# Row scores in four 32-row array tiles, and turned scores from operands stacked over 128 partitions

## What is computed

```python
q = jnp.einsum('bse,ef->bsf', layernorm(x), Wq)       # 32 heads of 16
k = jnp.einsum('bse,ef->bsf', ctx, Wk)                # 8 heads of 16, each serves 4 query heads
v = jnp.einsum('bse,ef->bsf', ctx, Wv)
q, k = rope(q), rope(k)
scores = jnp.einsum('bhqd,bhkd->bhqk', q, repeat(k, 4)) * 0.25
x = x + jnp.einsum('bhqk,bhkd->bhqd', softmax(scores), repeat(v, 4)) @ Wo
h = layernorm(x)
gate = softmax over the 16 best of (h @ Wq_w.T @ keys.T), spread over 64 experts
x = x + ((h @ A_w.T) * repeat(gate, 8)) @ B_w.T * 2
```

## Time and profile before

| | |
|---|---|
| median of three runs | 170.12 us |
| span of the profiled execution | 168.1 us |
| outside the span (170.12 less 168.1) | 2.0 us |
| TensorE busy | 97% of the span |
| TensorE weight loads busy | 77% |
| VectorE busy | 80% |
| ScalarE busy | 53% |
| GpSimd busy | 54% |

### The profile page before, as it was taken

The page is one execution under the profiler, slowest core; times in us unless marked ns, Lnnn a source line. Parts: engine busy times, 40 slices in busy tenths (PEclk is TensorE's granted clock), DMA queues, the critical chain, the costliest instruction groups (busy, mean ns, idle before and its releaser), DMA issues.

```text
span 168.1 us, 4082 instructions
## 1 busy us (share of the span) xinstructions
PE 162.7 (97%) x1437; PEld 129.9 (77%) x1437; DVE 134.9 (80%) x394; ACT 89.8 (53%) x212; POOL 91.1 (54%) x113
## 2 busy tenths in 40 slices
PE   7999999899999999999999999999999999999993
PEld 2657786678878787879887987879888866889883
DVE  1969886986998899799887998699884988767752
ACT  3588989899656362723538234732349154333210
POOL 5479999899799654805952099206440303512100
DMA  5999952313203010210212000100010001000013
GB/s 173 361 415 388 408 161 62 129 21 105 66 7 118 4 62 0 78 52 0 64 59 69 4 0 0 64 4 0 0 66 0 0 4 62 4 0 4 0 62 125
DMA packets 6739, 13.46 MB, mean 80 GB/s; under 512 B 832, under 2 KB 1216, under 8 KB 6464
## 3 DMA queue, kind: packets, MB, share of 16 engines
q1 hardware_dynamic: 6432, 12.95, 22.7%
q10 hardware_dynamic: 288, 0.27, 0.5%
HBM read 11.11 MB, written 2.10 MB: 79 GB/s over the span
## 4 chain that ended last, share of the span: by engine, by line
PE 52%; POOL 26%; issue 11%; DVE 5%; ACT 2%; DMA 2%; POOLq 0%; ACTq 0%; DVEq 0%
PE ps_w L1234 8%; PE ps_w L1235 7%; PE ps_w L1239 7%; PE ps_t L1247 4%; POOL am_lo L330 3%; POOL k_bd_hi L374 3%; POOL wo_lo L330 3%; PE ps_s L1320 3%; PE ps_s L1339 3%; POOL wq_lo L330 3%; POOL b_lo L330 2%; PE ps_t L1234 2%; PE ps_t L1239 2%; PE ps_t L1235 2%; POOL k_bd_lo L374 2%
## 5 line engine op out<-in xcount | busy, mean ns | idle before, releaser
L921 DVE TENSOR_REDUCE ps_s<-ps_s 128x8 f32<-128x512 f32 x32 | 21.0, 689 | 0.6 <-PE ps_s L1320 0.3
L398 POOL TENSOR_TENSOR late<-late,gate 128x512 f32<-128x512 f32 x7 | 7.6, 1084 | 24.2 <-issue 17.3
L383 POOL TENSOR_TENSOR oT_lo<-o_n,oT_hi 128x512 fp32r<-128x512 f32 x8 | 10.4, 1296 | 15.7 <-ACT oT_hi L611 15.7
L603 ACT ACTIVATE eT<-ps_s 128x512 f32<-128x512 f32 x32 | 17.0, 600 | 3.4 <-PE ps_s L1345 3.4
L1234 PE MATMUL ps_w<-am_hi,x2T_hi 128*128 128x288 f32 x48 | 14.3, 320 | 0.0
L1235 PE MATMUL ps_w<-am_lo,x2T_hi 128*128 128x288 f32 x48 | 13.1, 295 | 0.0
L1234 PE MATMUL ps_w<-b_hi,zT_hi 128*128 128x512 f32 (+1 forms) x28 | 10.7, 389 | 0.0
L1227 PE MATMUL ps_w<-wq_hi,xT_hi 128*128 128x512 f32 x26 | 10.7, 411 | 0.0
L1234 PEld LDWEIGHTS ps_w<-am_hi,x2T_hi 128*128 128x128 f32 x48 | 9.0, 187 | 2.1 <-ACT late L635 0.4
L1235 PE MATMUL ps_w<-b_lo,zT_hi 128*128 128x512 f32 (+1 forms) x28 | 10.4, 376 | 0.0
L653 ACT ACTIVATE zT_hi<-ps_t 128x512 fp32r<-128x512 f32 x7 | 4.2, 598 | 11.4 <-PE ps_t L1247 11.4
(11 more groups left out here) (256 smaller groups left out, 537.2 us busy)
## 6 DMA issues: line engine op xcount, KB each, us to landing
x_sb<-x SPq DMA_DIRECT2D x8, 256.0 KB, 6.7
cT_in<-cT SPq DMA_DIRECT2D x7, 256.0 KB, 2.8
out<-res SPq DMA_DIRECT2D x7, 256.0 KB, 2.0
wq_sb<-wq SPq DMA_DIRECT2D x4, 256.0 KB, 5.4
late<-wo SPq DMA_DIRECT2D x1, 1024.0 KB, 7.7
am_sb<-aT SPq DMA_DIRECT2D x1, 1024.0 KB, 8.8
b_sb<-bT SPq DMA_DIRECT2D x1, 1024.0 KB, 7.2
xT_raw<-xT SPq DMA_DIRECT2D x4, 256.0 KB, 2.9
```

Source lines behind the costliest of these rows:

```text
L383: pool.tensor_tensor(oT_lo[:], o_n[:].rearrange("p (b r q) -> p r b q", b=2, r=REP), oT_hi[:].bitcast(F32), ALU.subtract).then_inc(oT_lo_o ...
L603: act.activation(eT[:, c].rearrange("p b n -> p (b n)"), ps_s[:, c, :], ACT.Exp)\
L921: dve.tensor_reduce(neg_top[:, b, HALF_H * half:HALF_H * (half + 1), :], ps_s[:, 2 * (1 - b) + half, :].rearrange("p (r h k) -> p h r k", ...
```

## The change

Row scores of tiles 0 to 6 (`quad_rows`): each product takes 32 rows (two heads) and 128 columns, four side by side, 48 a tile. The maxima are then taken over both head pairs of all four banks, and all four reductions wait until the scores of both sequences are there. `neg_top` moves to bank 0, and the reciprocals of tiles 0 to 2 leave `ps_s` for `inv_late`.

Turned scores of tiles 3 to 6 (`STACKED`): DMAs copy the 32 rows of each pair into one 128-row operand (`q_stack`: high, high, low, and the maxima; `k_stack`: high, low, high, and `sel`), and one full-array product stands for four. `m_out` writes the maxima straight into rows 96 to 127 of `q_stack`, once for each b. `turn_m` comes two weight chunks earlier in `late_step`. The stacks lie where `am_sb` and `b_sb` were.

```diff
+            def stack_sel():                  # SyncE
+                sp.wait_ge(am_l, DK)
+                sp.wait_ge(sel_ok, 2)
...
+                        sp.dma_start(k_stack[3 * QUAD:P, s, c].bitcast(F32),
+                                     sel[rows].bitcast(F32))\
+                          .then_inc(st_sel, 16)
+            def stack_k(t):
+                sp.wait_ge(k_bd_ok, 2 * t + 2)
+                if t - 2 in STACKED:
+                    sp.wait_ge(sT_ps, t - 1)
+                for c in range(PAIRS):
+                    rows, at = slice(QUAD * c, QUAD * (c + 1)), 2 * (c % 2)
+                    for n, part in enumerate((k_bd_hi, k_bd_lo, k_bd_hi)):
+                        sp.dma_start(k_stack[QUAD * n:QUAD * (n + 1), t % 2, c].bitcast(F32),
...
+            def stack_q(t):
+                sp.wait_ge(qT_lo_ok, t + 1)
+                if t - 1 in STACKED:
+                    sp.wait_ge(sT_ps, t)
+                else:
+                    sp.wait_ge(b_l, DK)
+                for c in range(PAIRS):
+                    for n, part in enumerate((qT_hi, qT_hi, qT_lo)):
+                        sp.dma_start(q_stack[QUAD * n:QUAD * (n + 1), c]...
...
             load_xT(5)
+            stack_k(3)
+            stack_q(3)
             load_c(6)
+            stack_k(4)
             store(0)
             load_xT(6)
+            stack_q(4)
             load_c(7)
+            stack_k(5)
             store(1)
             load_xT(7)
+            stack_q(5)
+            stack_k(6)
+            store(2)
+            stack_q(6)
...
             def m_out(t):                     # ScalarE
+                if t in STACKED:
+                    for b in range(2):
+                        act.activation(q_stack[3 * QUAD:P, :, b, :],
+                                       mT_bank(t)[3 * QUAD:P, :].unsqueeze(1).broadcast_to([QUAD, PAIRS, 2 * P]),
+                                       ACT.Copy).then_inc(mT_ok, 1)
+                    return
...
             def top(t, b):                    # VectorE
+                if quad_rows(t):
+                    if b == 0:
+                        dve.wait_ge(s_ps, 2 * t + 2)
+                        if t >= 1:
+                            dve.wait_ge(m_lo_ok, t)
+                    for rp in range(2):
...
+            def quad_scores(t):               # TensorE
+                pe.wait_ge(qT_hi_ok, t + 1)
+                pe.wait_ge(qT_lo_ok, t + 1)
+                pe.wait_ge(k_bd_ok, 2 * t + 2)
+                if t >= 1:
+                    pe.wait_ge(exp_ok, 4 * t)
+                    if not late_tile(t - 1):
+                        pe.wait_ge(o_step, 3 * t - 2)
+                for b in range(2):
+                    for rp in range(2):
+                        for n, (q, k) in enumerate(((qT_hi, k_bd_hi), (qT_hi, k_bd_lo), (qT_lo, k_bd_hi))):
+                            for c in range(PAIRS):
+                                rows = slice(QUAD * c, QUAD * (c + 1))
+                                mm = pe.matmul(ps_s[:, c, at:at + P], q[rows, ...], k[rows, ...],
+                                               start=(n == 0), stop=(n == 2))
+                mm.then_inc(s_ps, 2)
...
+            def stacked_scores(t):
+                pe.wait_ge(st_q[t], 16 * 3 * PAIRS)
+                pe.wait_ge(st_k[t], 16 * 3 * PAIRS)
+                pe.wait_ge(st_sel, 16 * 2 * PAIRS)
+                for b in range(2):
+                    for c in range(PAIRS):
+                        if b == 0 and c in (0, PAIRS - 1):
+                            pe.wait_ge(mT_ok, mT_count(t) - (c == 0))
+                        mm = pe.matmul(ps_s[:, c, 2 * P * b:2 * P * (b + 1)], k_stack[:, t % 2, c, b, :],
+                                       q_stack[:, c, b, :], start=True, stop=True)
+                mm.then_inc(sT_ps, 1)
...
             def late_step(i):
-                up_high(f)
+                up_high(f, [0, 1])
                 turn_m(n)
+                up_high(f, [2, 3])
                 up_low(f)
```

More of the change, by code:

```diff
@@ L158, in build, with mT_count, quad_rows, neg_top_of @@
         ROUTE = ps_s[:, :, 0:E]
+        def mT_count(t):
+            return t + 1 + sum(1 for s in STACKED if s <= t)
+        def quad_rows(t):
+            return t < T - 1
+        def neg_top_of(t):
+            if quad_rows(t):
+                return ps_s[:, 0, 0:4 * KVH].rearrange("p (r b h) -> p b h r", b=2, r=2)
+            return ps_s[:, 2, 0:4 * KVH].rearrange("p (b h r) -> p b h r", b=2, r=2)
         def z_bank(t, half):
@@ L250, in build @@
         up_ps, res_ok, stored = sem("up_ps"), sem("res_ok"), sem("stored")
+        st_q = {t: sem(f"st_q{t}") for t in STACKED}
+        st_k = {t: sem(f"st_k{t}") for t in STACKED}
+        st_sel = sem("st_sel")
         block = ctx.enter_context(nc.Block())
@@ L309, in _ @@
             load_c(5)
+            stack_sel()
             load_x(7)
             load_xT(5)
+            stack_k(3)
+            stack_q(3)
             load_c(6)
+            stack_k(4)
             store(0)
             load_xT(6)
+            stack_q(4)
             load_c(7)
+            stack_k(5)
             store(1)
             load_xT(7)
-            for t in range(2, T - 1):
+            stack_q(5)
+            stack_k(6)
+            store(2)
+            stack_q(6)
+            for t in range(3, T - 1):
                 store(t)
@@ L1311, in scores @@
                 if t >= 1:
-                    if b == 0 or late_tile(t - 1):
+                    if b == 0:
                         pe.wait_ge(exp_ok, 4 * t)
                     else:
-                        pe.wait_ge(o_step, 3 * t if t < T - 1 else 3 * t - 2)
+                        pe.wait_ge(o_step, 3 * t - 2)
                 for rp in range(2):
@@ L1331, in turn_m @@
                 mm.then_inc(m_ps, 1)
+            def stacked_scores(t):
[3 more added lines that the diff above has]
+                for b in range(2):
+                    for c in range(PAIRS):
+                        if b == 0 and c in (0, PAIRS - 1):
[3 more added lines that the diff above has]
+                mm.then_inc(sT_ps, 1)
             def turned_scores(t):
-                pe.wait_ge(mT_ok, t + 1)
+                if t in STACKED:
+                    stacked_scores(t)
+                    return
+                pe.wait_ge(mT_ok, mT_count(t))
                 for b in range(2):
@@ L1452, in first @@
                 pe.wait_ge(route_ok, 1)
-                scores(0, 0)
-                scores(0, 1)
+                quad_scores(0)
                 turn_k(1)
@@ L1475, in second @@
                 turn_xh(3)
-                scores(1, 0)
-                scores(1, 1)
+                quad_scores(1)
                 pe.wait_ge(v_st_ok, 3)
@@ L1511, in step @@
                     project_q(p, [2])
-                scores(n, 0)
-                scores(n, 1)
+                quad_scores(n)
                 if f >= 0:
```

42 lines of the change are left out of this document (34 added, 8 removed).

## The result

The changed kernel takes 173.6 us (median of four runs, 171.2 to 174.0) where the kernel before takes 170.0 (169.7 to 170.4): a ratio of 1.016, with a 95% interval of 1.009 to 1.024. Two things are to be explained, since the profiled execution is the fastest of the four: it took 171.2 us (span 169.5) with a granted clock of 1.00 throughout, the other three 173.6 to 174.0 with a mean clock of 0.99.

The account below looks back on a forecast made before the run. TensorE was taken to bound the late steps, VectorE's maxima the early ones. -1.6 - 0.25 + 0.58 + 0.31 = -0.96 us from a 168.1 us span gave 167.1, plus 2.0 for the median: 169.1 us, range 168.3 to 169.9.

Parts of the forecast that it names:

- Behind it stand the turn of the maxima and the turned scores of tile 1: Tile 1, behind VectorE's maxima 0.31 us late: work that TensorE reached just as it came, so the delay counts.
- The maxima: VectorE's reductions wait for both sequences' scores: +0.58 us on tile 0, +0.31 on tile 1, nothing from tile 2 on.
- Stacked scores: Turned scores, tiles 3 to 6: eight full-array products take 0.95 us, not 1.35, without shape-change bubbles; -0.40 a tile, -1.6 us.
- Row scores: Tiles 0 to 6: groups at 0.112 us, bound by weight loads, save 0.08 us a tile; -0.25 us, tiles 4 to 6.
- The rival in which weight loads don't bind: Row scores: groups take 0.063 us, no late maxima on tiles 0 and 1; -3.6 us, 166.5 us; one in ten.
- its variant of 0.081: Row scores at the skill's 81 ns a matmul for N = 128: 167.4 us; no chance of its own given.
- The DMAs: SyncE's queue: issues of 0.46 us each, twelve in 5.5 us; tile 3's queries have 2.7 us of slack; nothing booked.
- I book nothing: SyncE, late steps: tile 7's input load issued near 92.5 instead of 87.16, wanted at 97.06; no cost counted.
- stacks come late: SyncE: slow SBUF-to-SBUF issues make tile 3's query stack late; at 0.8 us an issue 172.2 us; 13 in 100.
- the point x = 0.71: SyncE: DMA issue time in us from which late stacks eat the 1.0 us gained.
- The copies of the maxima: ScalarE: one copy becomes two of 1.03 us each, some 1.95 for both; covered by 0.3 us, so nothing.
- The sign that the prediction named for being wrong: Late steps: a new wait for maxima, ScalarE or a stack; alternatively, row-score groups coming at 0.06 us.

Follow-up runs that it names:

- the two runs with stacks alone: Changed kernel with row scores, maxima, reciprocals as before, only stacked products: 169.0 us, ratio 0.9953; with xT loads of tiles 6 and 7 earlier too: 168.9 us, 0.9942.
- the four-tile rows alone: Changed kernel without stacked products and their transfers, row scores of four 32-row products and reciprocals in SBUF kept: 172.6 us, ratio 1.0169 to the kernel before.
- the early loads alone: Changed kernel with only the loads of xT of tiles 6 and 7 earlier in SyncE's list: 172.3 us, ratio 1.0131 to the kernel before.
- the added GpSimd work: Changed kernel plus two GpSimd subtractions of 96x512 elements, SBUF to SBUF, beside tile 2's multiply: 173.8 us.
- the stretch filled: Changed kernel plus 8 useless TensorE products of a zero tile after tile 1's row scores, where it had waited 2.05 us for oT_hi: 171.7 us.

## Why the prediction was wrong, point by point

- **The step that failed** is one that the prediction doesn't have: the reciprocals' move to SBUF, an edit of three lines in the diff, was booked at nothing without a word. The sentence "Behind it stand the turn of the maxima and the turned scores of tile 1" left out what else stands there: VectorE's attend of tile 0, on which `oT_hi` hangs. What the runs showed in its place: TensorE waited 2.05 us for `oT_hi` and not 0.43, because VectorE's multiply of tile 0 took 2.19 us and not 0.75 beside GpSimd. The move measured +2.4 us by itself and 1.6 together with the rest of the change. The rule was in the Trainium skill (SBUF — State Buffer, SBUF: two separate sides): a VectorE instruction with two SBUF inputs and a GpSimd instruction that reads SBUF exclude one another for a whole instruction. The trace agrees: 2.26 us beside GpSimd, 0.76 without, and one multiply of a pair held up for about a whole GpSimd instruction.
- **The clock** had no term either. In most runs a stretch at the 1.2 GHz level adds 1.5 us or more, since TensorE stood still for 2 us.
- **The maxima** (+0.58 and +0.31): the mechanism and the first size were right (0.97 less 0.34). In all it is at most 1.3 us in the traces (0.6, and up to 0.7 behind it), for 0.9.
- **Stacked scores** (-0.40 a tile): right for the block, 0.95 us. Of the -1.6 us, 0.8 to 1.0 arrived by the ratios of the two runs with stacks alone; late loads, late stacks and, without the earlier `turn_m`, the copies of the maxima took the rest.
- **Row scores** (0.112 us a group, 0.08 a tile): right in mechanism, groups every 0.11 us, and 0.12 a tile measured. The rival in which weight loads don't bind (0.063) is refuted, and its variant of 0.081 too.
- **The DMAs**: mis-sized, 0.64 us an issue and not 0.46. "I book nothing" for the load of tile 7's input was wrong: it was issued at 97.6 us, not near 92.5, and the wait behind it cost 0.17 us here and 1.8 in another execution. The rival "stacks come late" named the resource, but in the changed kernel's profiled execution the load in the same queue was late, not the stack; the point x = 0.71 wasn't reached.
- **The copies of the maxima**: 1.93 us for two against 1.95, and hidden in the late steps, as forecast.

In all: 1.0 us of gain was forecast, with 0.9 of early loss in it. At full clock the early steps lose 2.9 us (2.3 in the table, 0.6 before it) and outweigh the gain, and the clock and the queue do the rest. The sign that the prediction named for being wrong, a new wait in a late step, came (0.22 and 0.17 us), but it is the small part of the miss. The single prices don't add up to the sum exactly, since they hide behind one another: the multiply and the wait for both sequences end in the same idle stretch.

## What to carry to other kernels

When an edit needs room and moves a small operand, list every instruction that reads it and ask in which memory each of its other operands lies; two operands in SBUF made VectorE's multiply 2.2 us long beside a busy GpSimd, and 0.76 beside an idle one. A gain in an engine's steady steps can be kept apart from a change of its early, dependent steps: take the part where nobody is awaited and leave the other. A queue that is filled with many small transfers makes every load behind them late, so put loads that others wait for ahead of them, and compare several runs, since one profiled execution showed neither the lower clock nor how much the queue's loss varies. Measure such a loss from start to start of the step: the wait that a row shows (0.22 us) was less than half of it.

## What the runs showed of the hardware that I had not expected

- Two 128x256 multiplies from SBUF took 2.2 us beside GpSimd's SBUF subtractions, 0.76 alone and 0.75 with one operand in PSUM.
- The granted clock fell to 0.50 after short idle stretches of TensorE: with 2.05 us idle in 18 of 20 runs of the four kernels that have such a stretch (the changed one, the four-tile rows alone, the early loads alone, the added GpSimd work), with 1.1 us in six of 32 runs of three kernels, and in none of six with the stretch filled. The stretch is read in one profiled execution of each kernel. In one execution the clock fell when TensorE was at work again and cost 1.5 us, in another it fell while TensorE was idle and cost 2.5.
- The issue of a 32-partition transfer from SBUF to SBUF took SyncE 0.60 us, where loads of 128 partitions took 0.33 to 0.46 in most rows.
